# Two loop bodies on VectorE for the expert blocks of a perceiver layer, and gathered rows transposed by tile height

## What is computed

```python
x = x + xattn(layernorm(x), ctx, ctx, ...)   # 16 heads, 8x64 queries, 1601 keys
x = x + attn(layernorm(x), ...)              # values have width HD - ROPE = 0: adds nothing
x = x + moe(layernorm(x), router_w, router_b, w1, b1, w2, b2)

def moe(x):                                  # 512 tokens, D 512, E 8 experts, H 2048, top 2
    logits = x @ router_w + router_b
    gating = softmax(where(in_top_2(logits), logits, -1e30))
    h = relu(einsum('td,edh->eth', x, w1) + b1[:, None, :])
    y = einsum('eth,ehd->etd', h, w2) + b2[:, None, :]
    return einsum('etd,te->td', y, gating)
```

## The kernel before, in words

| engine | in step c of a block | at the end of a block |
|---|---|---|
| TensorE | `hidden(c + 2)`: first product, high and low terms in two halves of a PSUM bank; then the second product of step c | in wide blocks `turn_outputs`: 8 transposes of `yt` |
| ScalarE | `h_part` = low terms + bias (line 908); `w_hi`, the high part of a quarter of the next weights (857, 865); `h_mix` high = relu of `h_sum` (914) | `gate_rows`: `y_gated` = outputs x gate (930), two instructions |
| VectorE | `h_sum` = high terms + `h_part` (line 1321); `w_lo`, the low part of the same weights (1209, 1217); `h_mix` low (1327) | bias of the next expert (1316), `sum_outputs`: 4 reductions into `yt` (1343) |
| SyncE | loads of weights, issued when the quarters of the buffer before are split | |
| GpSimd | | gathers the rows of the next block but one, adds outputs into `out` by indirect DMA |

## Time and profile before

### The profile page before, as it was taken

The page is one execution under the profiler, slowest core; times in us unless marked ns, Lnnn a source line. Parts: engine busy times, 40 slices in busy tenths (PEclk is TensorE's granted clock), DMA queues, the critical chain, the costliest instruction groups (busy, mean ns, idle before and its releaser), DMA issues.

```text
span 1131.3 us, 24023 instructions
## 1 busy us (share of the span) xinstructions
PE 1079.0 (95%) x7583; PEld 1029.5 (91%) x7584; DVE 1002.5 (89%) x2273; ACT 728.8 (64%) x1506; POOL 503.6 (45%) x447
## 2 busy tenths in 40 slices
PE   5999999999999999999999999998979999899996
PEld 4889999999999999999999999986868998789885
DVE  7789989989989899999999998988979888998995
ACT  3556666656565656565666666664668777787874
POOL 5556566657556665666475655261111121221211
PEclk9999999999999999999999999999889999999998
DMA  5321221222122212112212121044787877888883
GB/s 193 105 76 45 66 64 58 58 67 63 45 56 66 66 51 71 45 46 75 66 42 80 42 66 50 2 162 150 222 261 261 280 236 230 263 274 276 248 261 105
DMA packets 86366, 138.45 MB, mean 122 GB/s; under 512 B 15816, under 2 KB 40520, under 8 KB 86336
## 3 DMA queue, kind: packets, MB, share of 16 engines
q1 hardware_dynamic: 82800, 130.07, 35.9%
q0 software_dynamic: 3536, 8.00, 3.5%
HBM read 130.88 MB, written 7.17 MB: 122 GB/s over the span
## 4 chain that ended last, share of the span: by engine, by line
PE 74%; DVE 12%; issue 5%; ACT 5%; DMA 2%; DVEq 1%; POOL 0%; SPq 0%; ACTq 0%; POOLq 0%
PE ps L427 13%; PE ps L429 12%; PE ps L428 12%; PE ps L1489 8%; PE ps L1645 8%; PE ps L1539 8%; PE ps L1520 4%; PE ps L1521 4%; PE ps L1646 3%; DVE h_mix L1327 2%; DVE w_lo L1209 1%; DVE w_lo L1217 1%; DVE h_sum L1321 1%; DMA w_raw<-in_w_dram 1%; DVE qbd_lo L1110 1%
## 5 line engine op out<-in xcount | busy, mean ns | idle before, releaser
L581 POOL TENSOR_TENSOR ctx_hi<-ctx_raw,no_query 128x1152 fp32r<-128x1152 f32 x64 | 141.9, 2217 | 266.1 <-PE ps L429 255.4
L807 ACT ACTIVATE probs<-ps,negmax 128x1152 f32<-128x1152 f32 x64 | 78.4, 1225 | 184.9 <-DVE negmax L1140 184.9
L1037 DVE SCALAR_TENSOR_TENSOR k_mix<-ps,bk_sb,k_mix 64x384 fp32r<-64x384 f32 (+1 forms) x256 | 162.2, 634 | 32.2 <-ACT k_mix L767 27.1
L427 PE MATMUL ps<-wv_hi,ctx_hi 128*128 128x256 f32 (+1 forms) x624 | 180.7, 290 | 3.8 <-DVE k_mix L1037 3.7
L585 POOL TENSOR_TENSOR ctx_lo<-ctx_raw,ctx_hi 128x1152 fp32r<-128x1152 f32 x64 | 179.9, 2810 | 5.0
L429 PE MATMUL ps<-wv_hi,ctx_lo 128*128 128x256 f32 (+1 forms) x624 | 175.1, 281 | 0.0
L428 PE MATMUL ps<-wv_lo,ctx_hi 128*128 128x256 f32 (+1 forms) x624 | 174.7, 280 | 0.0
L1645 PE MATMUL ps<-xg_mix,w_hi 128*128 128x320 f32 (+1 forms) x584 | 157.5, 342 | 14.5 <-DVE h_sum L1321 7.6
L767 ACT ACTIVATE k_mix<-ps,bk_sb 64x384 fp32r<-64x384 f32 (+1 forms) x256 | 150.9, 589 | 25.7 <-PE ps L429 21.3
L1646 PE MATMUL ps<-xg_mix,w_lo 128*128 128x160 f32 (+1 forms) x584 | 135.2, 232 | 0.0
L427 PE MATMUL ps<-ctx_hi,wk_hi 128*128 128x384 f32 (+1 forms) x384 | 133.8, 348 | 0.0
(11 more groups left out here) (233 smaller groups left out, 2633.9 us busy)
## 6 DMA issues: line engine op xcount, KB each, us to landing
w_raw<-in_w_dram SPq DMA_DIRECT2D x76, 1024.0 KB, 5.5
ctx_raw<-in_ctx_t_dram SPq DMA_DIRECT2D x48, 576.0 KB, 3.8
ctx_raw<-in_ctx_t_dram SPq DMA_DIRECT2D x16, 673.5 KB, 4.1
out_dram<-acc POOLq DMA_DIRECT2D x2, 1024.0 KB, 10.8
q_both<-q_scratch SPq DMA_DIRECT2D x14, 128.0 KB, 3.0
x<-in_x_dram SPq DMA_DIRECT2D x4, 256.0 KB, 3.5
wq_raw<-in_wq_dram SPq DMA_DIRECT2D x1, 1024.0 KB, 7.8
q_scratch<-q_out SPq DMA_DIRECT2D x1, 1024.0 KB, 7.3
```

The costliest lines, as they stand in the source:

```text
L427: pe.matmul(acc_ap, a_hi, b_hi, start=start, stop=False)
L581: nc.gpsimd.tensor_tensor(ctx_hi[slot][:, :, 0:n], ctx_raw[slot][:, :, 0:n], no_query[:].rearrange("p (o i) -> p o i", o=1).broadcast_to([ ...
L1037: last = nc.vector.scalar_tensor_tensor(out=k_mix[other, 2 * a + i, cols], in0=ps[rows, bank, 0:m], scalar=bk_sb[rows, a:a + 1], in1=k_mix ...
```

## The change

VectorE gets a function `block_low(b, expert_next, n)` that is its old loop body, written twice: for n = 128 and for n = 160. Its loop now loads a second register (`is_narrow`) and branches. In the narrow body the additions into `h_sum` and the low parts of `h_mix` of steps 2 to 15 take 128 columns; the four reductions into `yt` are left out, and the semaphore `y_summed` is raised by 4 in their place. The columns 128 to 159 of `h_sum`, which ScalarE still reads, are cleared once by GpSimd. TensorE's `turn_rows` makes all 128-row transposes first and the 32-row ones behind them; `xg_turned` is raised at the same two places in count, both now among the last four.

```diff
@@ GpSimd, before the loop
             nc.gpsimd.memset(idx_next[:].bitcast(F32), 0.0).then_inc(rows_cleared, 1)
+            nc.gpsimd.memset(h_sum[:, :, P:BLOCK], 0.0).then_inc(rows_cleared, 1)
@@ VectorE
-            def sum_hidden(b, c):
+            def sum_hidden(b, c, n=BLOCK):
 
                 dve.wait_ge(h_parted, HT * b + c + 1)
-                nc.vector.tensor_tensor(h_sum[:, c % 4, :], ps[:, hidden_bank(c), 0:BLOCK], h_part[:, c % 2, :],
+                nc.vector.tensor_tensor(h_sum[:, c % 4, 0:n], ps[:, hidden_bank(c), 0:n], h_part[:, c % 2, 0:n],
                                         ALU.add).then_inc(h_summed, 1)
 
-            def relu_low(b, c):
+            def relu_low(b, c, n=BLOCK):
 
                 dve.wait_ge(h_high, HT * b + c + 1)
-                nc.vector.scalar_tensor_tensor(out=h_mix[:, c % 4, 1, :], in0=h_sum[:, c % 4, :], scalar=0.0,
-                                               in1=h_mix[:, c % 4, 0, :].bitcast(F32), op0=ALU.max,
+                nc.vector.scalar_tensor_tensor(out=h_mix[:, c % 4, 1, 0:n], in0=h_sum[:, c % 4, 0:n], scalar=0.0,
+                                               in1=h_mix[:, c % 4, 0, 0:n].bitcast(F32), op0=ALU.max,
                                                op1=ALU.subtract).then_inc(h_split, 1)
-            dve.wait_ge(rows_cleared, 2)
+            dve.wait_ge(rows_cleared, 3)
@@ VectorE's loop
-            with dve.Fori(0, blocks) as b:
-                expert_next = dve.value_load(table[0:1, bass.ds(b + 1, 1)], min_val=0, max_val=E - 1)
+            def block_low(b, expert_next, n):
+
                 for c in range(HIDDEN_AHEAD, HT):
-                    sum_hidden(b, c)
+                    sum_hidden(b, c, n)
...
                 take_bias(bass.ds(expert_next, 1))
-                sum_outputs(b)
+                if n == BLOCK:
+                    sum_outputs(b)
+                else:
+                    dve.sem_inc(y_summed, KD)
                 for c in range(HIDDEN_AHEAD):
                     sum_hidden(b + 1, c)
                     weight_low(b + 1, c)
                     relu_low(b + 1, c)
+
+            dve.wait_ge(narrow_ready, 1)
+            with dve.Fori(0, blocks) as b:
+                expert_next = dve.value_load(table[0:1, bass.ds(b + 1, 1)], min_val=0, max_val=E - 1)
+                is_narrow = dve.value_load(narrow[0:1, bass.ds(b, 1)], min_val=0, max_val=1)
+                with dve.If(is_narrow > 0):
+                    block_low(b, expert_next, P)
+                with dve.Else():
+                    block_low(b, expert_next, BLOCK)
@@ TensorE
             def turn_rows(b, moved):
 
                 pe.wait_ge(rows_moved, moved)
-                for half in range(2):
-                    for k in range(2):
-                        for u in range(BT):
-                            n, d = ROWS[u], slice((2 * half + k) * P, (2 * half + k + 1) * P)
+                for u in range(BT):
+                    n = ROWS[u]
+                    for half in range(2):
+                        for k in range(2):
+                            d = slice((2 * half + k) * P, (2 * half + k + 1) * P)
                             last = pe.transpose(ps[:, 4 + half, k * BLOCK + u * P:k * BLOCK + u * P + n],
                                                 xg_raw[0:n, u, d], ident[0:n, 0:n])
-                    last.then_inc(xg_turned, 1)
+                        if u == BT - 1:
+                            last.then_inc(xg_turned, 1)
```

More of the change, by code:

```diff
@@ L1399, in _ @@
                 w1_low_piece(1, piece)
-            with dve.Fori(0, blocks) as b:
-                expert_next = dve.value_load(table[0:1, bass.ds(b + 1, 1)], min_val=0, max_val=E - 1)
+            def block_low(b, expert_next, n):
                 for c in range(HIDDEN_AHEAD, HT):
-                    sum_hidden(b, c)
+                    sum_hidden(b, c, n)
                     if c == HT - 1:
-                        relu_low(b, c)
+                        relu_low(b, c, n)
                         gathered_low(b + 1)
```

## The result

The changed kernel takes 1136.37 us (median of 7 runs, 1134.64 to 1139.38), the kernel before 1132.29 us (median of 7, 1128.62 to 1132.97). The ratio is 1.0046, with an interval of [1.0035, 1.0058]: slower by over 0.2%. The forecast was 1133.9 us and "the same". The time lies in the range, but on the slow side.

The account below looks back on a forecast made before the run. Wide blocks were taken as bound by TensorE, narrow ones by a circle of waits over VectorE and ScalarE. Terms -2.0 - 1.6 - 2.4 - 0.2 + 7.8 = +1.6 us gave 1133.9 us against the median; range 1128.5 to 1137.8.

Parts of the forecast that it names:

- narrower sums: Steps 2 to 15 of narrow blocks: 128 columns instead of 160 save 0.50 us a block, -2.0 us over four.
- four reductions: VectorE in narrow blocks: of the 1.59 us they take, only 0.41 reach the path, four times, -1.6 us.
- transposes: TensorE in four wide blocks: eight with one height change take about 1.0 us instead of 1.58, -2.4 us.
- second load, seven edges: VectorE's added register load at each loop edge, priced at 0.75 us like the existing one.
- branch and jump, seven edges: VectorE at loop edges: branch not taken 0.12 us, taken 0.31, jump over a body 0.24.
- block 0: First block and its edge: cost and savings both vanish in TensorE's 5.09 us standstill, leaving -0.2 us.
- the circle over both engines: Narrow blocks: a loop of waits through VectorE and ScalarE, 3.32 us per two steps, sets the limit.
- the cheap edge: Rival: VectorE's sequencer starts under `w_lo`, so an edge costs 0.4 us and not 1.1, giving 1128.9; chance 0.15.
- VectorE as the only bound: Rival: in narrow blocks all its saved work counts, 2.5 us a block in place of 0.91, giving 1127.5; chance 0.12.
- The cold first jump: Rival: VectorE's first jump over its wide body takes as long as TensorE's 5.165 us, +3.7, 1137.6; chance 0.13.
- the time of 1154: Rival: VectorE stands 5 us fetching instructions at each of four later exits from a narrow body, +20 us; chance 0.03.
- The transposes save nothing: Rival: in wide blocks a 32-row transpose is slow by itself, so reordering gains nothing, +2.4, 1136.3; chance 0.12.

Follow-up runs that it names:

- reductions alone left out: Changed kernel with both register loads moved off the edge and narrow blocks kept at 160 columns, so only their four reductions are omitted: 1127.81 us, ratio 0.9963.
- a direct comparison: One body, load moved, new transpose order (1128.46 us) against reductions alone left out: narrow blocks 4 and 7 take 33.37 and 33.41 us, not 32.88 and 32.89.
- the load alone: Kernel before with a second register load at each loop edge, without branch or second body: 1142.17 us, ratio 1.0092.
- equal bodies: Changed kernel with both bodies at 160 columns and with the reductions, old transpose order; second load, branch and jump remain: 1143.77 us, ratio 1.0113.

## Why the prediction was right in range and wrong in size

Term by term, in the prediction's order:

| term | predicted | measured | from |
|---|---|---|---|
| narrower sums | -2.0 | 4 x -0.55 = -2.2 | stretches, reductions alone left out |
| four reductions | -1.6 | 4 x -0.4 = -1.6 | the rest of 0.96 for both; 0.5 each by a direct comparison |
| transposes | -2.4 | 4 x -0.70 = -2.8 | stretches without a fall of the clock; medians 1.7 (with falls of the clock), 3.0 and 3.1 |
| second load, seven edges | 5.25 (7 x 0.75) | +10.4 | the load alone, by the first `h_sum`; medians 10.0 |
| branch and jump, seven edges | 2.55 | +1.6 | equal bodies less the load alone, the same; medians 2.0 |
| sum with block 0 (-0.2, not measured) | +1.6 | +5.2 | measured in all: +4.1 by the medians, +5.2 by the ratio |

**The step that failed** is the price of the second register load. The prediction read 0.75 us for one load with its address operations from the one load that the trace had, and said that "the new one is of the same kind, so 0.75 more". The kind was right and the surroundings were not: the old load ended where the second scatter began, and the new one stands behind it. It measured 1.48 us, of which 0.76 are the scatter's hold (1.08 in place of 0.32). The sum of the edges, +7.8, was 12.0, and its upper end of +10 was too low. GpSimd's rows at the edge were never laid beside the sequencer's; they were in the trace of before, where the old load runs 982.53 to 982.84:

```profile
980.96 1.61 POOL L715 DMA_INDIRECT out_dram<-y_gated,idx_cur  x1 [14.92 <-ACT y_gated L930]
982.88 1.37 POOL L715 DMA_INDIRECT out_dram<-y_gated,idx_cur  x1 [0.30 <-issue]
```

A second load could only begin inside the second scatter, and an engine that was 45% busy over the span and 17% in a narrow block looked as if it could not matter.

That the time still fell into the range is partly luck: an edge 4.2 us too cheap stands against gains 0.6 too small, and the sum of the measured terms is itself 1.1 above the difference of the medians, which is within what medians of seven runs can tell. The stretches, forecast at about 33.6 and 37.5 us, came out at 34.0 and 38.1.

**Right**: that the circle over both engines, not VectorE's work, bounds narrow blocks (0.55 and not 0.93 a block); that of 1.59 us of reductions only the 0.41 of the relu's wait counts, or little more; that TensorE has no lead in step 4 of a wide block, so that a late edge is passed on whole (1.74 us there); and that block 0 hides its own edge (the waits for issue are at the seven other edges; there `h_sum` waits for `h_part`). The price of the branch and jump, 2.55 us for the 1.6 measured, was set too high: the argument that VectorE's operations are slower than TensorE's 0.087 and 0.169 us did not hold, since their rows take 0.05 us, and the jump is covered. The transposes saved 0.78 in place of 0.6 on the chain: one change of height costs less than the prediction kept for it.

**The rivals**: the cheap edge is out by the 12.1 us of waits, VectorE as the only bound by the stretches. The cold first jump, and with it the time of 1154, is out: no row of the new branch or jump took over 59 ns, and behind the first jump the sequencer stood 0.52 us, where it is 0.21 later. A rule of the Trainium skill (Runtime: NRT & Kernel Launch, Instruction fetch mechanics) says that a taken branch to outside the current window has to fetch. No pass here shows such a fetch, but the trace doesn't speak against the rule either: no run shows that a target in this loop, two bodies of some 100 rows each, lay outside the window. "The transposes save nothing" gave 1136.3, the measured time almost to the tenth, and was false all the same. A right number does not make a rival right; the experiment on that term does.

## What to carry to other kernels

Before an instruction is added at a place, look at what every other engine does in the same microsecond, GpSimd's indirect DMAs above all, even those of engines that are idle most of the time; a price read from one row holds for the surroundings of that row. A value that a branch needs at a loop's edge is loaded in the middle of the pass before, under a long instruction, into a register of its own: that turned +0.5% into -0.6% here. When a change is tried and comes out slightly slow, take it apart before it is dropped: three of its four parts were gains.

## What the runs showed of the hardware

**A register load of VectorE that begins 0.33 to 0.66 us into GpSimd's second scatter is held until the scatter is over.** In the three kernels of the argument (changed, equal bodies, two loads) it took 0.86 to 1.12 us in place of 0.30 to 0.32 and ended 0.02 to 0.17 us behind the scatter, at all 22 edges at which it stood there; it fell to 0.30 once the scatters were moved. Five more kernels show the same 35 times (the old order with two bodies, both loads moved, the reductions alone left out, and the two of one body with the load moved, whose load in step 2 takes up to 1.10 us). Not every meeting of the two is a hold: 16 loads that began 0.06 to 0.11 us ahead of the second scatter took 0.31 to 0.32 us beside it. Four, all the first load at the edge from block 0 to 1, began 0.17 to 0.19 us into it, took 0.72 to 0.73 and ended 0.45 us before its end. The loads in step 10, some of which began inside a gather of 1.1 us, took 0.31 to 0.32 us each. Why these differ is not settled, and no load lies inside the first scatter but for its last 0.07 us. The Trainium skill (SBUF — State Buffer, SBUF: two separate sides) tells of an exclusive lock on a port pair of VectorE and GpSimd, where the loser waits for the other's whole instruction. The wait until just behind the other's end looks like it, but here VectorE's own `w_lo` ran beside the scatter at its usual 1.21 us, and only the sequencer's load was held; no run here shows what it waits for.

**TensorE's clock falls to half for a few microseconds at edges, and where it does so differs from kernel to kernel.** In the profile of before, no stretch from 844 to 1122 us is below full clock; in the changed kernel there are two (980 to 984 and 1012 to 1018), in the one with the new transposes two (872 to 876 and 1012 to 1019), all near the end of a narrow block, where TensorE waits (1.3 us for one `h_sum` just before the spell at 1012). The equal bodies have two in the first steps of narrow blocks instead. In a narrow block it costs little (35.06 us with such a spell, 35.07 without); at the start of wide block 6 it cost 2.3 us (38.58 against 36.29). The order of the transposes seems to have a part in it. Of the eight kernels with the new order, seven show such a spell about an edge from a narrow block to a wide one; of the five with the old order none does there. In the two kernels of one body with the new order (load at the edge, load moved) blocks 2 and 6, which start in such a spell, take 37.04 us or more, and block 3 takes 36.2 to 36.3. Why the order would do this no run shows. One profile each does not say how often it happens; it is of the size of the spread between runs of one kernel.
